# A Mamba-2 block on one core: paired y_diag matmuls, one exponent bank, and orders of their own for both ends

## The reference

```
xn   = layernorm(x)
z, xBC, dt = split(xn @ W_in)                    # 512, 768, 8 columns
dt   = softplus(dt + dt_bias);  xBC = silu(causal_conv4(xBC))
xs, B, C = split(xBC)                            # 8 heads x 64, 128, 128
y    = ssd(xs * dt, -exp(A_log) * dt, B, C) + xs * D
y    = rmsnorm(y * silu(z)) * rms_w
attn = layernorm(xn + y @ W_out) * ln_g + ln_b
ffn  = tanh(xn @ W1 @ W2 @ W3 + bias)
out  = x + attn + ffn
```

## Time and profile before

| | before |
|---|---|
| median of 3 runs | 795.73 us (793.85 to 796.36) |
| the profiled execution | 797.4 us |
| its span, first to last instruction | 795.7 us |
| mean granted clock of TensorE | 0.985 |
| PE / DVE / ACT / POOL busy | 95% / 90% / 84% / 82% |
| HBM traffic | 11.45 MB read, 8.39 MB written |

### The profile page before, as it was taken

The page is one execution under the profiler, slowest core; times in us unless marked ns, Lnnn a source line. Parts: engine busy times, 40 slices in busy tenths (PEclk is TensorE's granted clock), DMA queues, the critical chain, the costliest instruction groups (busy, mean ns, idle before and its releaser), DMA issues. The chain is left out here.

```text
span 795.7 us, 19256 instructions
## 1 busy us (share of the span) xinstructions
PE 755.9 (95%) x5392; PEld 624.2 (78%) x5392; DVE 716.1 (90%) x1596; ACT 671.7 (84%) x1712; POOL 655.3 (82%) x1224
## 2 busy tenths in 40 slices
PE   4688999999999999999999999999999999999973
PEld 3567888888888888888888888888888888888853
DVE  3678999999999999999999999999999999999972
ACT  4687889889988888998888899988888998888851
POOL 4465898888888888888898888889888888888873
PEclk9899999999999999999999999999999999999996
DMA  6000000000000000000000000000000000000000
GB/s 194 0 15 1 16 27 28 28 28 14 12 26 26 26 26 26 25 1 26 26 26 26 26 26 0 26 26 26 26 26 26 4 22 26 26 26 14 14 14 27
DMA packets 21402, 20.14 MB, mean 25 GB/s; under 512 B 2816, under 2 KB 20864, under 8 KB 21376
## 3 DMA queue, kind: packets, MB, share of 16 engines
q1 hardware_dynamic: 19584, 19.67, 7.6%
q10 hardware_dynamic: 1792, 0.17, 0.2%
HBM read 11.45 MB, written 8.39 MB: 25 GB/s over the span
## 5 line engine op out<-in xcount | busy, mean ns | idle before, releaser
L644 DVE SCALAR_TENSOR_TENSOR u<-ring,cw,u 128x256 f32<-128x256 f32 x576 | 266.3, 476 | 18.7 <-ACT u L905 12.7
L1087 PE MATMUL ring<-xhl,wh 128*128 128x262 f32 x768 | 161.8, 304 | 7.0 <-issue 3.8
L1087 PE MATMUL ring<-wh,xhl 128*128 128x512 f32 (+1 forms) x512 | 152.1, 358 | 4.2 <-DVE u L644 2.2
L905 ACT ACTIVATE u<-ring,cb,cw 128x256 f32<-128x256 f32 x192 | 110.4, 575 | 41.2 <-PE ring L1087 41.2
L1087 PEld LDWEIGHTS ring<-xhl,wh 128*128 128x128 f32 x768 | 122.7, 193 | 17.0 <-issue 11.7
L1087 PEld LDWEIGHTS ring<-wh,xhl 128*128 128x128 f32 x512 | 89.9, 188 | 36.3 <-DVE u L644 23.1
L965 ACT ACTIVATE xdt<-xt_bank,dts 128x64 f32<-128x64 f32 x512 | 111.5, 335 | 0.0
L1087 PE MATMUL ring<-xhl,wl 128*128 128x262 f32 x384 | 110.6, 288 | 0.0
L1087 PE MATMUL ring<-wl,xhl 128*128 128x264 f32 (+1 forms) x256 | 86.8, 339 | 0.0
L664 DVE SCALAR_TENSOR_TENSOR lay<-e_bank,btg 128x512 f32<-128x512 f32 x128 | 86.3, 685 | 0.4 <-ACT e_bank L948 0.3
L948 ACT ACTIVATE e_bank<-e_bank 128x512 f32<-128x512 f32 x128 | 77.9, 609 | 0.8 <-PE e_bank L1182 0.4
(11 more groups left out here) (144 smaller groups left out, 2088.0 us busy)
## 6 DMA issues: line engine op xcount, KB each, us to landing
xin<-in_x_dram SPq DMA_DIRECT2D x32, 256.0 KB, 2.9
out_dram<-obuf SPq DMA_DIRECT2D x32, 256.0 KB, 2.9
lay<-in_w_in_dram SPq DMA_DIRECT2D x1, 776.0 KB, 8.5
lay<-in_w_in_dram SPq DMA_DIRECT2D x1, 512.0 KB, 9.3
wo<-in_w_out_dram SPq DMA_DIRECT2D x1, 512.0 KB, 10.3
lay<-in_f2t_dram SPq DMA_DIRECT2D x1, 256.0 KB, 5.6
lay<-in_f_dram SPq DMA_DIRECT2D x1, 256.0 KB, 6.2
lay<-in_f1t_dram SPq DMA_DIRECT2D x1, 256.0 KB, 8.8
```

Of the source, the lines that this page charges most:

```text
L644: v.scalar_tensor_tensor(out=u[:, ct], in0=conv_bank(ct)[:, :, t:t + P], scalar=cw[:, ct, t:t + 1], in1=u[:, ct], op0=ALU.mult, op1=ALU.ad ...
L905: s.activation(u[:, ct], conv_bank(ct)[:, :, HALO:PH], ACT.Identity, bias=cb[:, ct:ct + 1], scale=cw[:, ct, HALO:TAPS]).then_inc(u_done[ct ...
L1087: last = mul(out, a, c, start=first and i == 0, stop=i == n - 1)
```

## The change

What it does:

- PSUM: one exponent bank in place of two; two y banks, one for each q. exponents(q, half) now waits for the weigh of the quarter before. y_diag(k, q) waits for y_low of the step before of its own q only.
- y_diags: y_diag(k-1, 1) and y_diag(k, 0) stand next to one another on PE, once a pass.
- No y_off, scale_off, add_diag and decay_state for step 0 (new_state copies); no states, scale_x, decay_state and new_state for step 31.
- Setup is cut into units. `passes` becomes head(), the loop, tail(); each engine has a written out order for head and tail, with setup units between units of steps 0 to 3. The loop has a new order on each engine.
- Step 0 uses six banks for its six convolution blocks and xt_bank for the transposes of x.
- Loads: the columns of W_in for xBC and dt go second; the small loads f_bias, dt_bias, D and rms_w move from ACT's queue to SP's.
- For the last step the final normalisation is done for each q alone: end_scale on POOL, end_output on DVE; the store goes out in two halves.
- 14 matmuls on constants at the start of PE (warm).

```
-        e_bank0, e_bank1, xt_bank, bg_bank, yoff_bank, yd_bank = [
+        e_bank, xt_bank, bg_bank, yoff_bank, yd_bank0, yd_bank1 = [
...
-        def passes(eng, one_pass):
-            for k in range(-2, first):
-                one_pass(k, k % BUF)
+        def passes(eng, head, one_pass, tail):
+            head()
             with eng.Fori(first // BUF, last // BUF) as i:
                 for b in range(BUF):
                     one_pass(i * BUF + b, b)
-            for k in range(last, steps + 2):
-                one_pass(k, k % BUF)
-        def conv_bank(ct):
-            return (ring0, ring0, ring1, ring1, ring0, ring1)[ct][:, 0:Q * PH].rearrange("p (q t) -> p q t", q=Q)
+            tail()
+        def conv_bank(k, ct):
+            if at_start(k):
+                bank = (e_bank, xt_bank, bg_bank, yoff_bank, yd_bank0, yd_bank1)[ct]
+            else:
+                bank = (ring0, ring0, ring1, ring1, ring0, ring1)[ct]
+            return bank[:, 0:Q * PH].rearrange("p (q t) -> p q t", q=Q)
```

The exponent and y_diag units on PE:

```
             def exponents(k, q, half):
-                if at_start(k):
+                if at_start(k) and (q, half) == (0, 0):
                     pe.wait_ge(r_exp, 5)
+                    pe.wait_ge(tap_done[0], HALO)
                 pe.wait_ge(spread_done, 2 * (k + 1))
-                if begun(k - 1 + q):
-                    pe.wait_ge(m_done[1 - q][half], k + q)
+                if half == 1:
+                    pe.wait_ge(m_done[q][0], k + 1)
+                elif q == 1:
+                    pe.wait_ge(m_done[0][1], k + 1)
+                elif begun(k - 1):
+                    pe.wait_ge(m_done[1][1], k)
...
             def y_diag(k, q):
-                if begun(k - 1 + q):
-                    pe.wait_ge(ytl_done[1 - q], k + q)
+                if begun(k - 1):
+                    pe.wait_ge(ytl_done[q], k)
+                else:
+                    pe.wait_ge(tap_done[4 + q], HALO)
                 pe.wait_ge(xdt_done[q], k + 1)
                 for h in range(H):
                     if h % 4 == 0:
                         pe.wait_ge(m_done[q][h // 4], k + 1)
```

The new end of the last step:

```
+            def end_output(k, b, q):
+                dve.wait_ge(shift2_done, k + 1 + q)
+                v.tensor_scalar(hh[:, q], hh[:, q], rs2[:, q:q + 1], shift2[:, q:q + 1], ALU.mult, ALU.add).then_inc(hn_done[q], 1)
...
+                v.tensor_tensor(obuf[:, b, q], hh[:, q], lng[:, :], ALU.mult).then_inc(hg_done, 1)
...
+                v.tensor_tensor(obuf[:, b, q], obuf[:, b, q], res[:, b, q], ALU.add).then_inc(out_done, 1)
```

More of the change, by code:

```diff
@@ L565, in one_pass @@
+                if live(k):
+                    mask_g(k, 0)
+                    scale_x(k, b, 0)
+                if live(k - 2):
+                    output(k - 2, b1)
                 if live(k + 1):
-                    residual(k + 1, b1)
-                    spread_rows(k + 1)
-                if live(k):
-                    decay_state(k, b, 1)
+                    softplus(k + 1, b1, 0)
+                if live(k + 2):
+                    halo(k + 2, b2)
                 if live(k + 1):
-                    state_weights(k + 1, b1)
@@ L596, in _ @@
+            passes(pool, head, one_pass, tail)
         @block.vector
@@ L859, in _ @@
+            passes(dve, head, one_pass, tail)
         @block.scalar
@@ new lines, in left_table @@
+            def left_table(r):
+                if r == 0:
+                    act.wait_ge(s_const, 1)
+                rows_of, data = slice(r * LO, (r + 1) * LO), slice(r * LO, r * LO + Q * H)
+                s.activation(left[rows_of], pair[rows_of, r].unsqueeze(1).to_broadcast([LO, GROUPS, P]), ACT.Copy).then_inc(d_split, 1)
+                if r < 2:
+                    act.wait_ge(d_split, r + 1)
+                    act.wait_ge(s_member, 2)
+                    s.activation(left[data], member[data, :].unsqueeze(2).to_broadcast([Q * H, GROUPS, P]), ACT.Copy).then_inc(r_exp, 1)
+                elif r == QUAD - 1:
+                    act.wait_ge(d_split, QUAD)
+                    act.sem_inc(r_exp, 1)
@@ L947, in decay @@
                 act.wait_ge(e_in_psum[q][half], k + 1)
-                s.activation(e_bank[half][:, :], e_bank[half][:, :], ACT.Exp).then_inc(e_done[q][half], 1)
+                s.activation(e_bank[:, :], e_bank[:, :], ACT.Exp).then_inc(e_done[q][half], 1)
             def last_apply(k, q):
@@ L997, in _ @@
-            act.wait_ge(s_const, 1)
-            act.wait_ge(s_member, 2)
-            for r in range(QUAD):
-                rows_of, data = slice(r * LO, (r + 1) * LO), slice(r * LO, r * LO + Q * H)
-                s.activation(left[rows_of], pair[rows_of, r].unsqueeze(1).to_broadcast([LO, GROUPS, P]), ACT.Copy).then_inc(d_split, 1)
-                if r < 2:
-                    act.wait_ge(d_split, r + 1)
-                    s.activation(left[data], member[data, :].unsqueeze(2).to_broadcast([Q * H, GROUPS, P]), ACT.Copy).then_inc(r_exp, 1)
@@ new lines, in one_pass @@
+            def one_pass(k, b):
+                b1, bo = (b + 1) % BUF, (b - 1) % BUF
+                if live(k - 1):
+                    decay(k - 1, 0, 1)
+                if live(k):
+                    branch(k)
+                    softplus_exp(k)
+                    softplus_den(k)
+                if live(k - 1):
+                    x_times_dt(k - 1, bo, 1)
+                if live(k):
+                    conv_in(k, 2)
+                    conv_in(k, 0)
+                if live(k - 1):
+                    b_and_g(k - 1, 1)
+                    decay(k - 1, 1, 0)
+                if live(k - 2):
+                    square(k - 2, 0)
+                    square(k - 2, 1)
+                if live(k):
+                    conv_in(k, 3)
+                if live(k - 2):
+                    y_channels(k - 2, 1)
+                if live(k):
+                    conv_in(k, 1)
+                if live(k - 1):
+                    decay(k - 1, 1, 1)
+                if live(k):
+                    sums(k, b)
+                    conv_silu(k, b, 1)
+                    conv_silu(k, b, 0)
+                    z_silu(k, b, 0)
+                    conv_in(k, 4)
+                    conv_in(k, 5)
+                    x_times_dt(k, b, 0)
+                if live(k + 1):
+                    norm_apply(k + 1, b1)
+                if live(k):
+                    conv_silu(k, b, 2)
+                    z_silu(k, b, 1)
@@ L1066, in _ @@
+            passes(act, head, one_pass, tail)
         @block.tensor
@@ L1323 @@
+            passes(pe, head, one_pass, tail)
 def kernel(**inputs):
```

1449 lines of the change are left out of this document (1089 added, 360 removed).

## The result

The changed kernel takes **781.44 us** (median of 4 runs, 780.59 to 781.99) beside 795.48 for the kernel before in the same session: ratio 0.9827 [0.9803, 0.9851], 14.0 us faster. Forecast were 767.6 (757 to 781): the sign is right, the size is half, and the value lies just outside the range. The profiled execution took 780.59 us, its span is 778.9, 16.8 shorter than that of before.

A forecast was written before the change was run, and what follows sets the result against it. The prediction took TensorE, never idle, to bound the passes, and waits to decide head and tail. Savings of 6.7 (passes), 8.0 (head) and 13.4 (tail) sum to 28.1, so 795.7 - 28.1 = 767.6 us, range 757 to 781.

The forecast's parts named there:

- The reading of the bound: Passes: TensorE never idles, so only less work or fewer switches on it shorten them; VectorE close behind at 95.45%.
- The passes: 29 passes between sums(1) and sums(31): 22.80 each in place of 23.03, 6.7 us saved.
- The pair: Pass: two y_diag groups back to back save one pair of borders, 0.10 + 0.17 + 0.10 = 0.37 us.
- what the new order gives back: Pass: one fp32 states product between two fp32r projections costs 0.10 us, leaving 0.27 net.
- The head: Start to sums(2): followed along POOL, ACT and DVE, sums(2) at 69.5, 8.0 us saved, between 4 and 12.
- the cheaper price: Head: two more table loads on ACT at about 1.28 each, +2.6 us, where the skill page would give 5.3.
- The tail: Sums(31) to the end: chain walked to 37.0 in place of 50.35, 13.4 us saved, between 8 and 16.
- These closing terms: Tail after h and statistics: end_scale 1.6, three short DVE operations 1.3, store's issue to end 2.6 us.
- B: Rival, chance 0.18: the exponent bank and DVE's idle eat the border gain, passes stay 23.03; 774.3 us.
- the exponent bank: Pass: each quarter's exponent matmul, Exp and weigh, 2.0 us a turn, must finish first; cover at y_diag(k, 0) about 2.1.
- C: Rival, chance 0.08: the serial chain bounds the pass, kernel slower from a PE wait of about 1.0 per pass.
- D: Rival, chance 0.11: later constants and two table loads eat the head's gain, tail's gain kept; 775.6 us.

The follow-up runs named there:

- e17: Kernel before with two 512-wide products of the z projection left out (TensorE 0.46 less per pass): 795.54 us, ratio 0.9985.
- e2: Changed kernel with the two y_diag groups apart again in the loop passes, head and tail keeping their pairs: 791.77 us, ratio 0.9955.
- e16: Changed kernel with two 512-wide products of the z projection left out (TensorE 0.46 less per pass): 783.91 us, ratio 0.9846.
- e13: Changed kernel with TensorE's jump after y_off, GpSimd's mask earlier, last output halved, last projection in its own bank, ScalarE's C*B copy before step 31's first decay: 780.03 us.
- e9: Changed kernel with GpSimd's mask_g(k, 0) ahead of last_norm_scale(k - 2) in the loop passes: 779.67 us, ratio 0.9785.
- e3: Changed kernel with the last steps run in the pass's order, the whole last norm at once and one store: 787.72 us, ratio 0.9913.
- e4: Changed kernel, head only: Exp of A behind the high part on ScalarE, low_part before members on VectorE: 781.95 us, ratio 0.984.
- e5: Changed kernel without the 14 warm matmuls at the start of TensorE: 782.26 us, ratio 0.984.
- e7: Changed kernel, tail only: rms_scale(31) between the two operations of output(30) on GpSimd, last out projection written to xt_bank: 780.19 us, ratio 0.9817.
- e14: Changed kernel with the branch bias added to 16 of 264 columns only, so less VectorE work per pass: 782.1 us, ratio 0.9824.
- e19: Changed kernel with conv tile 1's last tap before VectorE's jump, GpSimd's mask earlier, TensorE's jump after y_off, last output halved, last projection in its own bank: 778.44 us.
- e6: Changed kernel with no hardware loops, the 27 middle passes written out on every engine: 779.92 us, ratio 0.9803.
- e10: Changed kernel without loops, with GpSimd's mask earlier, last output halved, last projection in its own bank, ScalarE's C*B copy before step 31's first decay: 778.89 us.
- c0: The control: the changed kernel run again as it is: 781.83 us, ratio 0.983.
- e1: Changed kernel with only TensorE's loop turned, its jump after y_off instead of before the exponents: 781.67 us, ratio 0.9827.

## Why the prediction went wrong, and where it was right

**The reading of the bound.** The step that failed is its first: "In the passes TensorE never idles, so only less work or fewer switches on it shorten them". e17 takes 0.46 of work off TensorE in the kernel before, and the pass doesn't shorten (23.02 in the mean of 29, for 23.03). Where the time is spent seems to matter: 0.38 more at the y_diag groups goes with a plain pass 0.51 longer (e2), 0.46 less in the z projection with no change (e16, e17). I read this as a period set by places where one engine waits for another (exponent, Exp, weighing; taps, projection); the shortest wait that the rows show is 0.15, and the modelled ends of matmuls cover shorter ones. Which chain is the longest stays open: cutting both engines at once wasn't tried, and neither was a cut on ScalarE or GpSimd, whose own lists are a rival that no run settles.

**The passes, 6.7 forecast, -2.7 measured.** The pair came out near its price (0.37; 0.40 by e2), but only in the mean: it is 0.51 in a plain pass and 0.17 in one with the turn, and e2 does not bring back the switch from fp32 to fp32r, which was 0.10 of the 0.37. The term that was mis-sized is what the new order gives back: 0.10 forecast, 0.35 measured (e2 against before), so that 0.05 of 0.23 is left. Over the 27 passes from sums(3) to sums(30) it is 0.8 us (621.39 for 622.18 before) where 6.2 were forecast, 5.4 short; two longer passes near the head, 23.46 and 23.50, are in it. One part of it can be seen: 0.17 came in a plain pass, but in the pass with the turn it is turned round, 23.25 for about 23.08. With two pairs of borders a turn cost at most 0.09 (0.05 in e2), with one it costs 0.40, and e13 and e9 show that more than one engine's jump is in it. The forecast had no term for a turn. Where the rest of the 0.35 comes from stays open. The first and the last of the 29 are the other 3.9 short: the head's and the tail's lists carry TensorE work over both landmarks, and I had counted 29 equal passes; e3, with the pass's order in the tail, has 23.01 for the last. By the Trainium skill ("TensorEngine Tiling (Array Packing)", Key Properties) a change of tiling mode drains the engine. e2 agrees: leaving the 64 wide mode takes 0.16 (1.02 for sixteen of 0.054) and entering it 0.09.

**The head, 8.0 forecast, 9.9 measured, 7.2 beside e17.** This walk held: first conv matmul 14.8 and 15.50, constants 13.5 and 13.85, sums(1) 45.0 and 44.19 (45.32 in the control), sums(2) 69.5 and 67.62. It missed that Exp of A waits for its load, which cost nothing (e4), since the constants held ScalarE behind it. The warm matmuls give nothing (e5). The price of a table load held too: here the ACTIVATE before it ends at 747.09, the load starts at 747.11, takes 1.28, and Exp starts at 748.40. By the Trainium skill ("ScalarE: Activation LUTs", What ACT_TABLE_LOAD costs) it would be 2.66 with its drain; the trace doesn't agree. sums(2) came 1.9 earlier than the cheaper price had it.

**The tail, 13.4 forecast, 9.6 measured, 7.8 beside e17.** First an addition: 32.2 + 1.6 + 1.3 + 2.6 is 37.7 and not 37.0, so the saving should have read 12.7 and the sum 768.3. These closing terms held (5.5; from 35.2 to 40.7 after sums(31)). What comes before them is 3.0 late: the walk was 1.7 early at the gate (26.7; TensorE reads it at 766.58, 28.4 after the landmark) and 3.2 early at the end of the last projection, of which 1.66 is the wait behind h. It had put the last rms scale on GpSimd without the output(30) ahead of it, and the first weighing without the mask (1.35). Removing the wait (e7) took 1.6 off the median but only 0.4 off the profiled tail, where TensorE was granted less clock; what it is worth at full clock stays open. The 50.35 that the saving is counted from was itself long, at a clock of 0.87, which the forecast did not price.

**The rivals.** B (passes stay) came nearest, at 774.3: the passes did stay, though its reason, the exponent bank, is not shown to be the bound; e14 shows a wait there. The time is 7.1 above B's: the 29 passes together got 2.7 longer, the tail gave 3.8 less than forecast and the head 1.9 more, and 2.8 of what the two profiles differ by is not in the medians. C's chain exists, but its price of 1.0 a pass didn't come: the four turns fit. D fell, the head gave all. 32 y_diag instructions in 1.90 was right.

## What to carry to other kernels

An engine shown busy at 100% isn't yet the bound: take a little work off it, if need be by leaving some out, and see whether the period moves; here neither engine's cut moved it, in either kernel. Cut in more than one place, since where the work sits can matter more than how much it is. Price a reordered loop body against a kernel with all edits but one, and count the pass with the loop's turn by itself. A landmark is only as good as the lists on both its sides: check the busy time between landmarks before calling the passes equal. And before a head or a tail is priced from one profile, read the granted clock of that stretch, and hold it against a second profile.

## What the runs showed of the hardware that was not expected

- **Loop turns.** The turn costs 0.40 us in the pass that has it, and 0.2 with TensorE's jump and GpSimd's mask moved off the waits (e13, e19). Written out (e6, e10) it is gone, but some passes are then 0.15 to 0.7 longer; two of them in each kernel have a gap of 0.44 or 0.45 on VectorE put down to issue. e6 is 1.9 us below the control; e10, with mask and tail edits too, 2.9.
- **The granted clock goes with the scatter.** Nine runs of the kernel before on one chip go from 792.56 us at a mean clock of 0.994 to 797.40 at 0.979. The falls lie in head and tail, where TensorE waits now and then: 1.2 us between sums(0) and sums(1) (c0); the tail of e13 is 3.3 longer than that of e9 (40.65, clock 0.96), with the swap's 0.9 in it. Such a fall needs no edit of the tail: from 30 to 34 us after sums(31) the changed kernel, c0 and e9 were granted 1.00, but e5, e1 and e6, with the same tail, 0.68, 0.77 and 0.77, and their tails took 42.28, 41.33 and 41.33 for 40.7. So the low clock behind the wait that e7 takes away need not be its doing.
